# A hand-scheduled attention and feed-forward kernel: how its first program block is joined to its second

## The reference

```
x = layernorm(x + softmax(q k' / 4) v @ wo)        # q, k, v = x @ wq, x @ wk, x @ wv
inter = x @ c1.T @ c2.T                            # rank 16, 1792 columns
idx = argmax of inter in each block of 32 columns  # 56 blocks
h = relu(w1[idx] . x);  out = sum over idx of h * w2t[idx]
x = layernorm(x + out)
```

## Time and profile before

| | us |
|---|---|
| median of 3 runs | 851.26 (850.18 to 851.35) |
| the profiled execution | 850.92 |
| its span in the trace | 848.9 |
| PE busy | 816.0 (96% of the span) |
| DVE busy | 622.4 (73%) |
| ACT busy | 388.4 (46%) |
| POOL busy | 292.1 (34%) |

### The profile page before, as it was taken

The page is one execution under the profiler, slowest core; times in us unless marked ns, Lnnn a source line. Parts: engine busy times, 40 slices in busy tenths (PEclk is TensorE's granted clock), DMA queues, the critical chain, the costliest instruction groups (busy, mean ns, idle before and its releaser), DMA issues. The chain is left out here.

```text
span 848.9 us, 11510 instructions
## 1 busy us (share of the span) xinstructions
PE 816.0 (96%) x4084; PEld 503.6 (59%) x4112; DVE 622.4 (73%) x804; ACT 388.4 (46%) x721; POOL 292.1 (34%) x388
## 2 busy tenths in 40 slices
PE   6999999999999999999989879999999999999995
PEld 5867433333333333333447657777777787777773
DVE  5588899999999999996036887558855795578554
ACT  4321788888888888887731022222112111122220
POOL 2212344654675465225303343342211222112221
PEclk9999999999999999999989989999999999999998
DMA  7783252344544453333225532210400040002001
GB/s 222 252 279 123 78 155 84 106 122 123 156 142 109 124 148 117 88 101 102 76 81 188 196 101 84 77 49 4 147 1 1 0 125 1 1 0 100 1 1 49
DMA packets 48224, 83.05 MB, mean 98 GB/s; under 512 B 9544, under 2 KB 13640, under 8 KB 48040
## 3 DMA queue, kind: packets, MB, share of 16 engines
q1 hardware_dynamic: 40448, 64.45, 24.5%
q0 software_dynamic: 7440, 16.76, 6.7%
q10 hardware_dynamic: 280, 1.11, 0.5%
HBM read 54.18 MB, written 28.05 MB: 97 GB/s over the span
## 5 line engine op out<-in xcount | busy, mean ns | idle before, releaser
L543 DVE TENSOR_REDUCE neg_max<-ps_pair 128x2 f32<-128x1024 f32 x256 | 301.4, 1219 | 30.6 <-PE ps_pair L641 30.6
L509 ACT ACTIVATE probs<-ps_st 128x512 f32<-128x512 f32 x512 | 265.8, 603 | 59.3 <-PE ps_st L654 58.3
L654 PE MATMUL ps_st<-q,k 50*128 50x512 f32 x512 | 185.0, 448 | 2.5 <-ACT probs L509 0.4
L654 PEld LDWEIGHTS ps_st<-q,k 50*128 50x128 f32 x512 | 83.4, 185 | 164.9 <-ACT probs L509 158.9
L892 POOL TENSOR_TENSOR g_l<-picked,g_h 128x512 fp32r<-128x512 f32 x56 | 73.0, 1303 | 250.5 <-ACT g_h L942 250.5
L641 PE MATMUL ps_pair<-k,q 48*128 48x512 f32 x512 | 149.1, 440 | 1.9 <-DVE neg_max L543 1.9
L668 PE MATMUL ps_pv<-probs,v 128*32 128x512 f32 x1024 | 136.4, 605 | 0.0
L935 ACT ACTIVATE picked<-ps_h 128x512 f32<-128x512 f32 x56 | 33.5, 598 | 182.4 <-PE ps_h L1156 182.4
L999 DVE STREAM_TRANSPOSE turned<-ps_prep 128x512 f32<-128x512 f32 x56 | 40.0, 715 | 93.3 <-PE ps_prep L1131 93.3
L1156 PE MATMUL ps_h<-xt_h,w_h 128*128 128x512 f32 x224 | 87.9, 392 | 0.5 <-ACT picked L935 0.5
L1156 PE MATMUL ps_h<-xt_l,w_h 128*128 128x512 f32 x224 | 87.5, 391 | 0.0
(11 more groups left out here) (141 smaller groups left out, 1174.6 us busy)
## 6 DMA issues: line engine op xcount, KB each, us to landing
operands<-parts POOLq DMA_DIRECT2D x20, 512.0 KB, 3.7
q<-operands SPq DMA_DIRECT2D x64, 128.0 KB, 2.5
sums<-stage SPq DMA_DIRECT2D x32, 256.0 KB, 3.1
x_raw<-xT SPq DMA_DIRECT2D x16, 256.0 KB, 5.0
k<-operands SPq DMA_DIRECT2D x64, 64.0 KB, 2.3
q<-operands SPq DMA_DIRECT2D x64, 64.0 KB, 2.6
att<-sums SPq DMA_DIRECT2D x16, 256.0 KB
yf<-x SPq DMA_DIRECT2D x4, 1024.0 KB, 5.4
```

What stands on the lines that cost most here:

```text
L509: nc.scalar.activation(probs[kt % 2][:, r], ps_st[i % 3][:], ACT.Exp, scale=float(HD) ** -0.5).then_inc(exp_done, 1)
L543: nc.vector.tensor_reduce(neg_max[:, at:at + 2], ps_max[pair % 2][:], AX.X, ALU.max, negate=True).then_inc(max_red, 1)
L654: nc.tensor.matmul(ps_st[i % 3][:], k_[n % QR][64 * a:64 * a + ROWS, kt * P:(kt + 1) * P], q[n % QR][64 * a:64 * a + ROWS, j, :], start=Tr ...
```

## The change

Batch 0's residual and statistics move from the head of the second block to the end of the first (`project_out` there now signals each tile, and the semaphores and `stats` are handed on). The waits for `stage` leave the end of the first block and stand ahead of the load of `den`. There are three residual buffers; batch b uses `y[b % 3]`, batches 1 and 2 load theirs without a wait, and batch 3's goes into batch 0's. On PE, `inner_up(0, 0)` and `first_marks(0, 0)` move ahead of batch 3's projections, and the marks of slot 1 between them. DVE's and POOL's lists are put in an order to match.

```
@@ -266,10 +266,7 @@
             store_unit(NU - 1)
-            for j in range(2):
-                sp.wait_ge(stage_out[j], NU // 2 * DMA)
             sp.wait_ge(rden_out, DMA * (NB - 1))
-            sp.wait_ge(y0_in, DMA)
@@ -555,6 +552,12 @@
+            def add_residual(t):
+                dve.wait_ge(wo_done, t + 1)
+                nc.vector.tensor_tensor(y0[:, t], ps_max[t // 2][:, t % 2], y0[:, t], ALU.add).then_inc(added, 1)
+                dve.wait_ge(added, t + 1)
+                nc.vector.bn_stats(stats[:, t], y0[:, t]).then_inc(stat_done, 1)
@@ -599,6 +602,9 @@
+            dve.wait_ge(y0_in, DMA)
+            for t in range(TT):
+                add_residual(t)
@@ -744,8 +753,7 @@
-        y = [y0, sb("yf1", [P, TT, D])]
+        y = [y0, sb("yf1", [P, TT, D]), sb("yf2", [P, TT, D])]
@@ -822,11 +829,10 @@
             def load_residual(b):
-                if b >= 2:
-                    sp.wait_ge(x1_out, DMA * (b - 1))
-                if b == 2:
+                if b == 3:
+                    sp.wait_ge(x1_out, DMA)
                     sp.wait_ge(prep_mm, TT)
@@ -842,6 +848,8 @@
+            for j in range(2):
+                sp.wait_ge(stage_out[j], NU // 2 * DMA)
             sp.dma_start(den[:], last.rearrange("(n h d q t) -> n h d q t", n=NH, h=2, d=HD, t=P)[:, 1, 0]
@@ -909,18 +917,19 @@
             root(0)
+            scale()
             root(1)
-            scale()
             for r in range(REP):
                 low_att(r)
             root(2)
             low_w2(0)
-            root(3)
             for b in range(NB):
                 for m in range(MT):
                     low_g(b, m)
                     if b == 0 and m + 1 < MT:
                         low_w2(m + 1)
+                    if (b, m) == (0, 0):
+                        root(3)
@@ -1056,36 +1064,38 @@
-            add_residual(0, 0)
-            add_residual(0, 1)
+            variance(0)
+            norm(0)
             dve.wait_ge(den_in, DMA)
             nc.vector.reciprocal(inv_den[:], den[:]).then_inc(inverted, 1)
-            add_residual(0, 2)
-            add_residual(0, 3)
-            variance(0)
-            norm(0)
...
             front(U)
+            add_residual(2, 0)
+            add_residual(2, 1)
             front(marks(0))
-            add_residual(2, 0)
             norm(1)
-            for t in range(1, TT):
+            for t in range(2, TT):
                 add_residual(2, t)
             variance(2)
+            pick(0, 0)
             norm(2)
-            for t in range(TT):
-                add_residual(3, t)
+            add_residual(3, 0)
+            add_residual(3, 1)
+            front(marks(1))
+            add_residual(3, 2)
+            add_residual(3, 3)
             variance(3)
...
-                    if (b, m) == (0, 0):
+                    if (b, m) == (0, 1):
                         norm(NB - 1)
@@ -1197,26 +1207,28 @@
-            for t in range(TT):
-                project_out(3, t)
             inner_up(0, 0, (0, 1, 2, 3))
+            first_marks(0, 0)
+            project_out(3, 0)
+            project_out(3, 1)
+            front(marks(1))
+            project_out(3, 2)
+            project_out(3, 3)
```

More of the change, by code:

```diff
@@ L70, in _overlays, with _attend @@
         return w_raw, w_h, w_l, x_raw, x1, v_rows, parts
-def _attend(nc, x, xT, w_qkv, wo, c1, c2, w1, dram, overlays, keep, late):
+def _attend(nc, x, xT, w_qkv, wo, c1, c2, w1, dram, overlays, keep, late, passed):
     sums, operands, maxima, rden = dram
@@ L78, in _attend @@
     att_parts2, y0, ps_max = late
+    stats, wo_done, added, stat_done, y0_in, stage_out = passed
     att_h, att_l = zip((xt_h[1], xt_l[1]), (xt_h[0], xt_l[0]), att_parts2)
@@ L680, in project_out @@
                     r, (a, w) = i // 3, ((att_h, wo_h), (att_h, wo_l), (att_l, wo_h))[i % 3]
-                    nc.tensor.matmul(ps_max[t // 2][:, t % 2], a[0][:, r, t * P:(t + 1) * P], w[:, r],
-                                     start=(i == 0), stop=(i == 11))
+                    last = nc.tensor.matmul(ps_max[t // 2][:, t % 2], a[0][:, r, t * P:(t + 1) * P], w[:, r],
+                                            start=(i == 0), stop=(i == 11))
+                if third == 2:
+                    last.then_inc(wo_done, 1)
             for o in range(TASKS):
@@ L711, in _, with _feed_forward @@
             weigh(NU - 1, TT - 1)
-def _feed_forward(nc, x, x1, out, w2, w2_late, sums, rden, keep, late):
+def _feed_forward(nc, x, x1, out, w2, w2_late, sums, rden, keep, late, passed):
     w1_h, w1_l, c1_h, c1_l, c2_s, ident, ident16, first, xt_h, xt_l, u, wo_h, wo_l = keep
@@ L853, in _ @@
             load_w2(1)
+            load_residual(3)
             store(1, flat(x1, 1), y[1], x1_out)
-            load_residual(3)
-            store(2, flat(x1, 2), y[0], x1_out)
+            store(2, flat(x1, 2), y[2], x1_out)
             for b in range(NB):
@@ L861, in _ @@
                     if (b, m) == (0, 1):
-                        store(NB - 1, flat(x1, NB - 1), y[1], x1_out)
+                        store(NB - 1, flat(x1, NB - 1), y[0], x1_out)
                     first_slot = 0 if b else 1
@@ L1022, in add_residual @@
             def add_residual(b, t):
[L1023 to L1026, removed]
+                dve.wait_ge(y_in[b % 3], DMA)
+                dve.wait_ge(wo_done, TT * b + t + 1)
+                nc.vector.tensor_tensor(y[b % 3][:, t], ps_out[t][:], y[b % 3][:, t], ALU.add).then_inc(added, 1)
                 dve.wait_ge(added, TT * b + t + 1)
-                nc.vector.bn_stats(stats[:, t], y[b % 2][:, t]).then_inc(stat_done, 1)
+                nc.vector.bn_stats(stats[:, t], y[b % 3][:, t]).then_inc(stat_done, 1)
             def add(b):
-                dve.wait_ge(y_in[0], DMA * (NB // 2 + b))
+                dve.wait_ge(y_in[0], DMA * (2 + b))
                 dve.wait_ge(out_mm, MT * (b + 1))
@@ L1085, in _ @@
                     steps = slot_steps(b, m)
-                    if steps:
-                        step(*steps[0])
-                    pick(b, m)
+                    if b * MT + m:
+                        if steps:
+                            step(*steps[0])
+                        pick(b, m)
                     if len(steps) > 1:
@@ L1199, in _ @@
             project_out(2, 3)
-            for t in range(TT):
-                project_out(3, t)
             inner_up(0, 0, (0, 1, 2, 3))
+            first_marks(0, 0)
[4 more added lines that the diff above has]
+            project_out(3, 3)
             for b in range(NB):
                 for m in range(MT):
+                    if b * MT + m == 0:
+                        continue
                     steps = slot_steps(b, m)
                     before = divmod(b * MT + m - 1, MT)
-                    if b * MT + m:
-                        inner_up(b, m, (0, 1))
+                    inner_up(b, m, (0, 1))
                     if steps:
                         step(*steps[0])
-                    if b * MT + m:
-                        inner_up(b, m, (2, 3))
+                    inner_up(b, m, (2, 3))
                     first_marks(b, m)
-                    if b * MT + m:
-                        inner_down(*before, (0, 1))
+                    inner_down(*before, (0, 1))
                     if len(steps) > 1:
                         step(*steps[1])
-                    if b * MT + m:
-                        inner_down(*before, (2, 3))
+                    inner_down(*before, (2, 3))
             inner_down(NB - 1, MT - 1, (0, 1, 2, 3))
@@ L1250, in build @@
         late = att_parts2, y0, [ctx.enter_context(nc.psum_tensor(f"ps_pair{j}", [P, 2, S], F32)) for j in range(2)]
-        _attend(nc, x, xT, w_qkv, wo, c1, c2, w1, (sums, operands, maxima, rden), overlays, keep, late)
-        _feed_forward(nc, x, x1, out, w2, w2_late, sums, rden, keep, late)
+        sem = lambda name: ctx.enter_context(nc.semaphore(name))
+        passed = stats, sem("wo_done"), sem("added"), sem("stat_done"), sem("y0_in"), [sem(f"stage_out{j}") for j in range(2)]
+        _attend(nc, x, xT, w_qkv, wo, c1, c2, w1, (sums, operands, maxima, rden), overlays, keep, late, passed)
+        _feed_forward(nc, x, x1, out, w2, w2_late, sums, rden, keep, late, passed)
 def kernel(L0_attn_x, L0_attn_wq, L0_attn_wk, L0_attn_wv, L0_attn_wo, L0_ffn_c1_w, L0_ffn_c2_w, L0_ffn_w1,
```

22 lines of the change are left out of this document (10 added, 12 removed).

## The result

The changed kernel takes 862.67 us (median of 4 runs) against 851.18 before: ratio 1.0141, 95% interval 1.0122 to 1.0160. The forecast was 855.7, in a range of 850.5 to 858.5. The sign came out, and so did the wait for the reloaded tile; the size didn't: +11.5 instead of +4.5, and some 5 of the 11.5 have a cause that the forecast hadn't.

A forecast was written before the change was run, and what follows sets the result against it. PE, busy 96%, was taken as the bound, fixed by its first reloaded tile, which hangs on batch 3's norm. +2.1 us for that tile and +2.4 for slow clock gave +4.5: 855.7 us, range 850.5 to 858.5.

The forecast's parts named there:

- the wait for the reloaded tile: PE in slot (0, 2) waits about 8 us, until 506.3, 8.0 behind norm(3)'s end; before, 504.18 without a wait.
- The boundary: Between the blocks: PE resumes at 437.1 instead of 439.39, the 2.6 us of slow clock go; PE 4.9 us ahead.
- Norm(2) beside three subtractions: Batch 2's norm on DVE, crowded by three POOL subtractions at 0.95 each: 4.8 us, ending at 482.5.
- the Trainium skill's lock: DVE's fast forms and POOL lock each other out: up to 1.3 per subtraction, norm(2) 1.0 more, sum 856.7.
- VectorE's chain from batch 2's first add to the end of norm(3): DVE from 465.0 through adds, marks, picks and norms to norm(3)'s end at 498.3, against 496.2 before.
- the landing of store(0) and of the residual behind it: SP's queue: store(0) lands at 462.4, batch 2's residual is complete at 465.0, against 468.0 before.
- TensorE's wait ahead of the first marks: PE stands at 466.7 before first_marks(0, 0) and waits for the mask to 471.4.
- The "worse" variant: Queued loads also hold up att and the store, 1 us or two, or slow clock costs more: 857 to 858.5.
- The smaller clock term: Behind PE's long wait for the reloaded tile the clock is down; forecast loss 2.4 us.
- From there on both kernels run the same list: From PE's first transpose of a reloaded tile, slot (0, 2), at 504.18, whatever is late is paid in full.
- The faster one: Residual in by 459.7 and POOL not holding norms up: norm(3) ends at 488.3, time 845.8; chance 0.10.
- The no-change rival: DVE's norms go through and POOL gives way: norm(3) ends at 493.5, time 851.0; chance 0.16.

The follow-up runs named there:

- e12: Kernel before with batch 0's adds in attention's last units and the waits behind the boundary, two buffers, old orders, stats at the end of SBUF: 850.57 us, ratio 0.9989.
- e4: Changed kernel with stats behind w1_h and w1_l, batch 1's reload waiting for store(1) alone, ahead of store(3): 851.88 us, ratio 1.0008.
- e8: Changed kernel with stats of 128 bytes a partition, marks(0) ahead of batch 2's adds, batch 1's reload waiting for store(1) alone: 850.34 us, ratio 0.9996.
- e6: Changed kernel with stats of 128 bytes a partition, batch 2's residual and the w2 loads behind it again waiting for store(0): 859.72 us, ratio 1.0109.
- e9: Changed kernel with stats behind everything else in SBUF, all TensorE operands at the addresses of before: 857.28 us, ratio 1.0070.
- e2: Kernel before with 96 unused bytes per partition ahead of w1_h and w1_l, no instruction changed: 855.77 us, ratio 1.0046.

## Why the prediction was wrong in size and right in its course

**Right.** The boundary: TensorE's first matmul at 438.0, 1.1 of it the execution's own, against 437.1 forecast, with the clock at 1.00; e12 shows that of this gain, taken by itself, 0.5 us (0.2 to 1.7) of the 4.9 reaches the end by the medians. Norm(2) beside three subtractions: 4.84 measured, 4.8 forecast; the Trainium skill's lock (SBUF — State Buffer, Who interferes with whom) was reckoned at 1.0 more, and the row doesn't show that. VectorE's chain from batch 2's first add to the end of norm(3): 32.7 measured, 33.3 forecast. TensorE's wait for the reload: 7.2 measured, about 8 forecast, 7.2 instead of 8.0 us behind the norm. That this is the gate, e4 and e8 show with 8.7 and 8.5 us.

**Wrong in size: the landing of store(0) and of the residual behind it.** The step reckoned that "about 8 of the 16 engines work" and put what the new loads on the other 8 cost those at nothing: store(0) at 462.4, the residual at 465.0. Measured, less the 1.1: about 465.8 and 468.5, 3.5 us late. TensorE's wait ahead of the first marks, 7.2 instead of 4.7, comes from the same delay. The queues from 458 to 462 (packets, MB, share of 16 engines), against the last of the earlier trace rows:
```profile
q1 hardware_dynamic: 469, 0.90, 103.8%
```
Before, 416 packets took 52.8% (the time of about 8 engines); after, 469 took 103.8% (of all 16). Each packet took 1.7 times as long, and hardly more was moved: 0.90 MB instead of 0.82. So the packets kept their pace only as long as no loads ran beside them. e6 shows the cause by taking the loads away, and that even then the residual comes no earlier than 467.6: a whole 1 MB then has to come behind the store. The "worse" variant had this mechanism, with "1 us or two". With +2.9 for the end of norm(3), -0.8 for the shorter way to the tile and +1.6 instead of +2.4 for the clock (+5.8 less the transposes' +4.2), the passage lost 5.8 instead of 4.5 in this execution. The smaller clock term is this execution's luck: in e9 it was the forecast 2.4, and by the medians, e9 against before, the order costs 6.2.

**Wrong because left out: the addresses.** The sentence "From there on both kernels run the same list" was taken to mean that they run it equally fast. The part on the change never priced the allocation of `stats` ahead of `w1_h`. It costs 4.1 us in after's trace, 4.5 by e2 and 5.3 by e9 against after (+11.5 less +6.2). This term takes the time out of the range: the order without it, 857.3, lies inside.

**The rivals.** The faster one decides with a norm(3) that ends before 492; it ended at 502.3. The no-change rival needed norms that POOL gives way to; 4.84 is against it. In the faster rival's sum the 14.1 us are 13.9 by the same durations; nothing hangs on that.

## What to carry to other kernels

A reload that waits for all stores together hangs on the last of them: give it the one store that it reads, before working on anything ahead of it. A load that starts earlier beside transfers that others wait for must be priced by what it takes from these, also where they leave half of the DMA engines idle. And a new tensor goes to the end of SBUF, or the addresses of all matmul operands behind it move, which cost 2.6 to 4.1 us here without a wait in the profile.

## What the runs showed of the hardware

The time of identical matmuls depends on where their operands stand in SBUF. The loss over the some 50 slots behind the passage: all as before 0.0 us; the second stage's tensors 96 bytes on +2.6; `w1` and all behind it 96 on +4.1; 128 on +3.1. A median start to start of 227 ns became 234 to 235 with the shift of 96. Which pair of addresses matters, and by what rule, stays open.

The packets of SP's queue, of 2 KB nearly all, took 0.08 to 0.10 us on average between 454 and 462 in before, where the time of about 8 engines was used, and 0.17 and then 0.14 in after, where the loads ran beside the sums and store(0). What these share isn't settled. It isn't a total of 0.2 MB/us: from 465.2 to 466.0 in before, loads alone moved 0.37 to 0.47 MB/us. An issue of a 1 MB load behind these transfers took SP's queue 5.93 us (at 448.63 in after), one at 439.92 only 0.58.
